# A recurrence on Trainium2: products of 56 columns in place of 8 and filler, and powers asked for two slots ahead

## What is computed

```python
def block(x, t_emb, ...):                     # x += block(x)
    xn = layer_norm(logmap0(x)); xm = expmap0(xn * (1 + sc_msa) + sh_msa)
    q, k, v = (_to_heads(plin(xm, w, b)) for w, b in ...)       # 16 heads of 16
    attn = softmax(einsum('bhqd,bhkd->bhqk', logmap0(q), logmap0(k)) / 4)
    out_h = expmap0(einsum('bhqk,bhkd->bhqd', attn, logmap0(v)))
    attn_out = plin(_from_heads(out_h), w_o, b_o)
    x = mobius_add(residual, expmap0(g_msa * logmap0(attn_out)))
    ... ff = plin(plin(xm, w_f1, b_f1), w_f2, b_f2)             # 256 -> 1024 -> 256
    return mobius_add(residual, expmap0(g_mlp * logmap0(ff)))

def lstm(x, h0, Wx, Wh, b):                   # x += lstm(x), h0 = cond
    xW = einsum('ntd,dk->tnk', x, Wx) + b
    def step(carry, xw_t):
        prev_h, prev_c = carry
        a = xw_t + prev_h @ Wh
        i, f, o = sigmoid of its first three quarters; g = tanh of the fourth
        next_c = f * prev_c + i * g
        next_h = o * tanh(next_c)
```

## Time and profile before

| | |
|---|---|
| Median of 3 executions | 1766.14 us (1760.43 to 1796.03) |
| Profiled execution, time | 1792.91 us |
| Its span, first to last instruction | 1791.2 us |
| Mean granted TensorE clock | 0.801 |
| PE, PEld, DVE, ACT, POOL busy | 88, 71, 67, 52, 26% |

### The profile page before, as it was taken

How to read it: one execution, slowest core, us unless ns; L and a number is a source line. 1 busy time by engine, 2 the same in 40 slices (tenths; PEclk the granted TensorE clock), 3 DMA queues, 4 the chain that set the end, 5 groups by cost and what they waited for, 6 DMA issues and landing times.

```text
span 1791.2 us, 64180 instructions
## 1 busy us (share of the span) xinstructions
PE 1570.5 (88%) x24605; PEld 1269.0 (71%) x24605; DVE 1196.0 (67%) x6690; ACT 933.0 (52%) x3335; POOL 457.9 (26%) x1246
## 2 busy tenths in 40 slices
PE   3656567768799999999999999999999999999998
PEld 3545445446687778787878787877787777878776
DVE  6455567666567767677677777676557666675665
ACT  0333457766446656566566665665344544544433
POOL 4222211121231424142424233232404133140100
PEclk9676665556888867677688887789689999998999
DMA  7000000000000000000000000000000000000000
GB/s 235 0 0 0 0 1 1 1 1 1 5 2 9 3 8 3 8 3 9 3 8 3 9 3 8 3 9 3 8 2 9 9 3 8 3 6 5 3 6 5
DMA packets 16704, 18.29 MB, mean 10 GB/s; under 512 B 6036, under 2 KB 15384, under 8 KB 16408
## 3 DMA queue, kind: packets, MB, share of 16 engines
q1 hardware_dynamic: 13016, 10.51, 2.1%
q10 hardware_dynamic: 3392, 3.81, 0.7%
HBM read 12.21 MB, written 2.10 MB: 8 GB/s over the span
## 4 chain that ended last, share of the span: by engine, by line
PE 58%; DVE 17%; ACT 5%; issue 4%; POOL 2%; DVEq 0%; ACTq 0%; POOLq 0%
PE psum L784 24%; PE psum L828 14%; PE psum L760 4%; PE psum L732 3%; PE psum L725 3%; PE psum L660 3%; DVE weights L1152 2%; DVE cnew L1389 2%; ACT ot L1004 2%; PE psum L774 2%; DVE hl L1398 2%; PE psum L740 2%; DVE hl L1396 2%; DVE gO L1384 2%; POOL sc L464 2%
## 5 line engine op out<-in xcount | busy, mean ns | idle before, releaser
L784 PEld LDWEIGHTS psum<-hl,wh 128*128 128x128 f16 x16384 | 490.7, 98 | 137.4 <-DVE hl L1398 121.4
L784 PE MATMUL psum<-hl,wh 128*128 128x8 f16 x16384 | 520.6, 172 | 27.3 <-DVE hl L1398 8.9
L828 PE MATMUL psum<-zeros,ident 128*128 128x256 f16 x2534 | 388.2, 296 | 5.9
L998 ACT ACTIVATE tA<-gA 128x16 f32<-128x16 f32 x512 | 110.4, 216 | 509.2 <-DVE gA L1380 509.2
L828 PEld LDWEIGHTS psum<-zeros,ident 128*128 128x128 f16 x2534 | 244.2, 105 | 82.4 <-issue 20.1
L1380 DVE TENSOR_REDUCE gA<-psum 128x16 f32<-128x32 f32 x512 | 97.1, 190 | 222.9 <-PE psum L784 217.8
L1152 DVE TENSOR_TENSOR weights<-w,weights 128x256 f16<-128x256 f32 x512 | 201.1, 417 | 17.3 <-ACT weights L901 16.9
L907 ACT ACTIVATE w<-psum 128x512 f32<-128x512 f32 x256 | 154.6, 604 | 27.7 <-DVE weights L1152 26.0
L901 ACT ACTIVATE weights<-psum 128x512 f16<-128x512 f32 x256 | 154.1, 602 | 16.9 <-PE psum L672 16.8
L1396 DVE TENSOR_TENSOR hl<-ot 128x8 f16<-128x8 f32 x512 | 89.8, 175 | 92.4 <-ACT ot L1004 90.7
L1004 ACT ACTIVATE ot<-cnew 128x8 f32<-128x8 f32 x512 | 109.6, 214 | 74.1 <-DVE cnew L1389 14.9
(11 more groups left out here) (301 smaller groups left out, 2412.3 us busy)
## 6 DMA issues: line engine op xcount, KB each, us to landing
arena<-in_x_dram SPq DMA_DIRECT2D x4, 512.0 KB, 9.9
wf<-in_L_cond_w_f_dram SPq DMA_DIRECT2D x2, 1024.0 KB, 17.6
xr<-in_x_dram SPq DMA_DIRECT2D x64, 32.0 KB, 1.8
out_dram<-place SPq DMA_DIRECT2D x64, 32.0 KB, 1.6
qTs<-in_L_cond_w_ada_dram ACTq DMA_DIRECT2D x1, 1536.0 KB
oT<-in_L_cond_Wh_dram ACTq DMA_DIRECT2D x1, 1024.0 KB, 14.5
wx<-in_L_cond_Wx_dram SPq DMA_DIRECT2D x1, 1024.0 KB, 18.1
rows<-in_L_cond_b_ada_dram ACTq DMA_DIRECT2D x4, 128.0 KB, 14.1
```

The lines of the kernel that those rows point to most:

```text
L784: last = mm(cols, wh16[:, half, kc, (g0 + c) * P:(g0 + c + 1) * P], hl[:, :, kc, :, 2].rearrange("p e b -> p b e"), start=False, stop=c == ...
L828: mm(pF[:, D:2 * D], ident16[:], zeros[:], start=False, stop=False, skip_group_check=True)
```

## The change

- A step's 32 products stream 56 columns (WIDE = 7 times 8). `hl` is now the middle of `hlz`, 13 blocks of 48 halves, of which all but the seventh stay zero. `state` gives the moving operand as seven blocks of 8 columns, of which the first (`first`) or the last is the state and six are zeros; the output takes 56 adjacent columns of the bank, so that zeros are added to other steps' or the filler's columns. Its order within a block is batch, then half: steps of 3 and of 24 elements.
- `keep_busy` counts the step's products as 1792 columns and wants 2800. The rule for the first four steps goes. Score products count 256 instead of 512. Fillers read the first 256 columns of `hlz`.
- Merges 0 to 7: the head powers are asked for at r = 3 (before, 2) and taken at r = 5; the row power is asked for at r = 5 (4) and taken at r = 7. `ask_for` adds to the semaphore and does not wait. The scaling into oS is at r = 8 instead of 7, for all merges.
- osq and nfrow become parts of tmp; zeros goes.

`head_slot` is not touched by the diff.

```diff
-WANTED, FIRST_STEPS = 2900, 4000
+WANTED = 2800
...
+        hlz = sb("hlz", [P, (2 * WIDE - 1) * BLOCK], F16)
+        hl = hlz[:, (WIDE - 1) * BLOCK:WIDE * BLOCK].rearrange("p (e k b s) -> p e k b s", e=2, k=KD, b=B)
...
                 if k < 2 * B:
-                    if r == 2:
+                    if r == 3:
                         powers((num("rh", H), num("smx", H), HALF_DOWN, H))
-                    if r == 4:
+                    if r == 5:
                         powers((one("cbm"), one("cam"), HALF_DOWN, 1))
...
+            def state(kc, first):
+
+                at_ = (WIDE - 1 if first else 0) * BLOCK + kc * B * 3 + 2
+                one_ = hlz[:, at_:at_ + 1]
+                return bass.AP(one_.tensor, one_.offset, [one_.ap[0], [BLOCK, WIDE], [3, B], [KD * B * 3, 2]])
...
                 for c in range(w):
-                    cols = gate_cols(which, r)[:, c * B:(c + 1) * B, :]
+                    at_ = (r * w + c) * B * 2
+                    first = at_ + WIDE * B * 2 <= 512
+                    low = at_ if first else at_ - (WIDE - 1) * B * 2
+                    cols = bk[:, low:low + WIDE * B * 2].rearrange("p (x b e) -> p x b e", x=WIDE, b=B)
                     for kc in range(KD):
                         for half in range(2):
-                            last = mm(cols, wh16[:, half, kc, (g0 + c) * P:(g0 + c + 1) * P], hl[:, :, kc, :, 2].rearrange("p e b -> p b e"),
+                            last = mm(cols, wh16[:, half, kc, (g0 + c) * P:(g0 + c + 1) * P], state(kc, first),
...
-                cols, us = 264 * (t - 5 in HEAD_AT) + 512 * (t in HEAD_AT), 0.33 * (t - 5 in HEAD_AT) + 0.45 * (t in HEAD_AT)
+                cols, us = 264 * (t - 5 in HEAD_AT) + 256 * (t in HEAD_AT), 0.33 * (t - 5 in HEAD_AT) + 0.45 * (t in HEAD_AT)
...
-                count = int(min((WANTED - 256 - cols) / D, (1.3 - us) * 2400 / D))
-                if t < 4:
-                    count = (FIRST_STEPS - 256 - cols) // D
+                count = int(min((WANTED - 32 * WIDE * B * 2 - cols) / D, (1.3 - us) * 2400 / D))
...
-                    mm(pF[:, D:2 * D], ident16[:], zeros[:], start=False, stop=False, skip_group_check=True)
+                    mm(pF[:, D:2 * D], ident16[:], hlz[:, 0:D], start=False, stop=False, skip_group_check=True)
...
+            def ask_for(what, last):
+
+                nonlocal asked
+                asked += 1
+                answer[what] = asked
+                last.then_inc(s["q_in"], 1)
...
-                if r == 2:
+                if r == 3:
...
-                    ask(d.tensor_scalar(num("smx", H), num("ssn", H), 1.0, None, ALU.max))
+                    ask_for(("heads", k), d.tensor_scalar(num("smx", H), num("ssn", H), 1.0, None, ALU.max))
+                if r == 5:
+                    v.wait_ge(s["m_now"], k + 1)
+                    ask_for(("row", k), d.tensor_scalar(one("cam"), one("now"), 1.0 / (HEAD * HEAD), TINY, ALU.mult, ALU.max))
+                    v.wait_ge(s["q_out"], answer[("heads", k)])
                     link(d.tensor_scalar(num("fr", H), num("rh", H), REACH, 1.0, ALU.mult, ALU.min))
                     link(d.tensor_tensor(num("fd", H), num("fr", H), F("rd"), ALU.mult))
-                if r == 4:
-                    v.wait_ge(s["m_now"], k + 1)
-                    ask(d.tensor_scalar(one("cam"), one("now"), 1.0 / (HEAD * HEAD), TINY, ALU.mult, ALU.max))
+                if r == 7:
+                    v.wait_ge(s["q_out"], answer[("row", k)])
                     link(d.tensor_scalar(one("sow"), one("cbm"), REACH, 1.0, ALU.mult, ALU.min))
...
-                if r == 7:
+                if r == 8:
                     v.wait_ge(s["m_F"], k + 1)
```

More of the change, by code:

```diff
@@ L76 @@
 SETTLE = 12
+WIDE = 7
+BLOCK = 48
 HEADS = B * NB * H
@@ L166, in bass_hyperbolic_block_then_lstm @@
         mv1 = sb("mv1", [P, 2])
-        nfrow = sb("nfrow", [1, P])
         c0T = sb("c0T", [P, KD, B])
@@ L178, in bass_hyperbolic_block_then_lstm @@
         w32 = sb("w32", [P, 4, T])
-        zeros = sb("zeros", [P, D], F16)
         uo = sb("uo", [P, 2, D])
-        osq = sb("osq", [P, D])
         oS = sb("oS", [P, D])
@@ L200, in bass_hyperbolic_block_then_lstm @@
         tmp = sb("tmp", [P, FF])
+        osq = tmp[:, 3 * D:4 * D]
+        nfrow = tmp[:, 0:P]
         xn = sb("xn", [P, D])
@@ L204, in bass_hyperbolic_block_then_lstm @@
         wh = oT[:, :, :, :, :, :].rearrange("p a k w b t -> p (a k w b t)").rearrange("p (k n) -> p k n", k=KD)
-        v32 = osq[:].rearrange("p (h e) -> p h e", h=H)
+        v32 = osq.rearrange("p (h e) -> p h e", h=H)
         c0R = usq[:].rearrange("p k (b t) -> p k b t", b=B)
@@ L209, in bass_hyperbolic_block_then_lstm @@
         c0 = xn[0:B, :]
-        hl = sb("hl", [P, 2, KD, B, 3], F16)
+        hlz = sb("hlz", [P, (2 * WIDE - 1) * BLOCK], F16)
+        hl = hlz[:, (WIDE - 1) * BLOCK:WIDE * BLOCK].rearrange("p (e k b s) -> p e k b s", e=2, k=KD, b=B)
         gA = sb("gA", [P, 16])
@@ L914, in merged @@
                         act.wait_ge(s["m_ss"], k)
-                    A(osq[:], uo[:, k % 2, :], ACT.Square).then_inc(s["m_sq"], 1)
+                    A(osq, uo[:, k % 2, :], ACT.Square).then_inc(s["m_sq"], 1)
                 if r == SETTLE:
@@ L1016, in _ @@
             d.memset(ot3[:], 0.0).then_inc(s["dinit"], 1)
-            d.memset(hl[:], 0.0).then_inc(s["dinit"], 1)
+            d.memset(hlz[:], 0.0).then_inc(s["dinit"], 1)
             v.wait_ge(s["dinit"], 2)
             d.memset(hl[:, 0, :, :, 0], -1.0).then_inc(s["dinit"], 1)
-            d.memset(zeros[:], 0.0).then_inc(s["dinit"], 1)
+            d.memset(num("spare"), 0.0).then_inc(s["dinit"], 1)
             v.sem_inc(s["l_lo"], 1)
@@ L1179, in ask @@
                 v.wait_ge(s["q_out"], asked)
+            answer = {}
+            def ask_for(what, last):
[3 more added lines that the diff above has]
+                last.then_inc(s["q_in"], 1)
             def merged_ahead(k, r):
                 F = lambda name: num(name, 2 * H)[:, k % 2 * H:(k % 2 + 1) * H]
-                if r == 2:
+                if r == 3:
                     v.wait_ge(s["m_ss"], k + 1)
@@ L1205, in merged @@
                         v.wait_ge(s["m_mn"], k)
-                    d.tensor_reduce(num("ssh", H), by_head(osq[:]), axis=AX.X, op=ALU.add).then_inc(s["m_ss"], 1)
+                    d.tensor_reduce(num("ssh", H), by_head(osq), axis=AX.X, op=ALU.add).then_inc(s["m_ss"], 1)
                 if r == 4:
```

## The result

| | before | after |
|---|---|---|
| Median of 4 executions each | 1776.31 us (1760.43 to 1796.03) | 2500.11 us (2499.21 to 2501.75) |
| Ratio of the times, 95% interval | | 1.4118 (1.3982 to 1.4254) |
| Profiled execution, time | 1792.91 us | 2499.21 us |
| Its mean granted clock | 0.801 | 0.639 |

The kernel became 41% slower where 1730 us and a gain were forecast. The page of after: first its busy times and the granted clock of 40 slices, then two groups (busy us, mean ns of one, idle time before it and what ended that), the recurrence's products and DVE's wait for them. Line 795 is line 784 of before.

What follows compares the result with a forecast made beforehand. The prediction took the recurrence's step loop (1315 of 1791 us) as the bound, with fillers delaying steps at half clock. Sum: 1792.9 - 24 - 90 + 45 + 10 - 4 gives 1730 us; range 1672 to 1778.

Steps and rivals of the forecast that it cites:

- Wider products, pitch: Recurrence's 32 products: 56 columns stay hidden behind the 27 ns pitch at full clock, cost 0; +0.56 us a step at half.
- rival 1: Recurrence's products: the strided read is slow, 46 ns a product at either clock, kernel slower at 1997 us; chance 0.17.
- the ring: Each recurrence step's serial cycle: about 1.0 us of PE products, then 1.3 us of DVE and ACT before the next products.
- Upper bound for the pitch: Recurrence's products: at most 46 ns each at full clock, if the strided read goes at half speed.
- Wider products, last result: End of each step's products: DVE gets the last column 20 ns later at full clock, +10 us over 512 steps.
- Half clock: Recurrence loop: 90 us lost to fillers at half clock goes; +45 returns, mainly in 195 slots with only 2560 columns.
- rival 2: Recurrence loop: full clock throughout, carried by the columns streamed before light slots; 1685 us, chance 0.15.
- rival 3: Recurrence loop: two thirds of 195 light slots stay at half clock, 86 us instead of 45, 1771 us; chance 0.18.
- Merges: Slots before step 0: asking POOL for powers two slots ahead shortens DVE's wait, -24 us, bounds 8 to 31.
- Power no earlier: Slots before step 0: the waiting only moves to another request on POOL, 1754 us; chance 0.05.
- Fewer fillers: Last slot of each round's gate work: two fillers no longer stand before the products, -4 us over 16 slots.
- free: Merges and set-up: moving the oS scaling one slot later, sharing tmp and replacing two memsets by one cost nothing.

Runs made afterwards that it cites:

- pairs4: Changed kernel with high and low halves side by side, 32 columns per product instead of 56, more fillers from their own zeros; 1675.61 us, ratio 0.9418 to before.
- runs: Changed kernel with state pairs 32 bytes apart, read as 4 runs of 14 neighbours, output written in adjacent pairs; 1763.41 us, ratio 0.9789 to before.
- adjacent_zeros: Changed kernel with products reading 56 adjacent zeros instead of the state, the recurrence's product left out of the result; 1697.83 us.
- spread: Changed kernel with state values 16 bytes apart, zeros between, read as 8 runs of 7, output strided in PSUM; 2072.22 us, ratio 1.162 to before.
- merges_only: Changed kernel with the old 8-column products and old fillers, keeping the merges' later requests and takings; 1778.62 us, ratio 0.9985 to before.

## Why the prediction was wrong, point by point

- **Wider products, pitch: the step that failed.** It was argued that 56 columns are 24 ns at full clock and hidden, from fillers and from products of 33 columns. All of these read adjacent numbers, so they had no say on a read that is spread. The term was 0 and measured +46.2 ns x 31 = 1.43 us a step, 732 us in all. The doubt was priced as rival 1 but played down with DVE's strided reads the earlier trace rows, and the half argument was a wrong one: what counted were TensorE's own reads. In its place the runs showed a read of 73.2 ns for 56 columns in this order, at either clock, against 26.2 for adjacent ones; a price of 1.8 to 1.9 ns for each 16-byte piece newly touched where pieces are taken one after the other; and layouts of the operand that bring the pitch back under 27 ns (pairs4, runs).
- **Rival 1** had the mechanism and the sign (chance 0.17), and its point of decision, 31 ns. Its price was too low: 0.82 ns a column was borrowed from streaming at half clock, which the read does not follow. Measured: 73.2/56 = 1.3. With the measured 1.50 us a step in its sum, 1792.9 - 24 - 4 - 90 + 768 = 2443. Of the 56 us to 2499 some 46 are side work that stood out over the ring in heavy steps (88 us over light steps, where the sum kept 132 - 90 = 42), 6 the merges, and 4 the gain from fewer fillers, which stands in the sum and not in the ledger.
- **Upper bound for the pitch**: set at 46 ns by the nearest row, it was no bound. 8 columns hidden under 27 ns only limited a column to 3.4 ns. That looser bound, 56 x 3.4 = 190 ns, was the only one that rows gave for such a read, and it was not used.
- **Wider products, last result**: +10 forecast at 0.02 us a step. After: 0.07 a step, +36, by the slow read (the mean record went from 172 to 243 ns). With an adjacent read (adjacent_zeros) about 0.
- **Half clock**: the loss of before, 90, is about right (pairs4's loop is 101 us shorter; 20 are left in adjacent_zeros). Its return in light slots was mostly in the right place (32 of 43 steps in adjacent_zeros) and over-sized, 20 for 45; so between the forecast and rival 2 (1685), not towards rival 3. In after itself it could not be seen: 441 steps saw half clock, the opposite of "over 0.95 in heavy slots". A step of 3.8 us holds the columns of one of 2.3, but so do the steps of 3.1 us of spread, which kept full clock; why after lost it is open.
- **Merges**: -24 forecast, -18 measured in after and -16 alone, within its 8 to 31. DVE's wait is 1.5 us each (10.7/7; 1.2 forecast) and the second one gone (0.2); it stood before L1196, where the prediction writes L1195. The sum took for granted that the gain reaches the kernel's time; merges_only has a ratio of 0.9985.
- **Power no earlier** fell with these rows. **Fewer fillers** (-4) and **free**: no run tells these apart.

## What to carry to other kernels

A matmul operand read in steps had a price of its own here, paid per 16-byte piece of SBUF rather than per column, higher when the order goes back and forth between pieces, and invisible until it passed the pitch of the weight loads. Before widening a product, count the pieces of its read, look at their order and at that of its write (pairs of adjacent fp32 columns were free, single ones not), and choose the layout by that. A row of an adjacent read, or of another engine, says nothing about it. Where no row shows an access, the only honest bound is the slack in which it is now hidden.

## What the hardware showed unexpectedly

- TensorE reading fp16 from SBUF: 1.8 to 1.9 ns for each 16 bytes newly touched, the same at both clock levels (56 columns 8 halves apart: 101.6 and 101.9 ns).
- Alternating between two such pieces with every column costs 73 ns for 56 columns, more than the 51 of as many columns from the same pieces in a kinder order.
- TensorE writing fp32 to PSUM at full clock: single columns 32 bytes apart 0.87 ns each (48.8 ns for 56); pairs 32 bytes apart are hidden (26.4 ns).
- A pair of LDWEIGHTS and MATMUL with 56 adjacent columns is no slower than one with 8 strided ones: 26.2 against 26.9 ns.
- DVE: a scan of 24 numbers 208 ns and 263 ns with its result 32 bytes apart; a product of 8 numbers 175 and 198 ns.
